# Six-layer local attention and MLP on one core: the third up-projection moved from slot 2 to slot 3, and the down-projection later in slot 3

## What is computed

```python
def local_attention(q, k, v):      # 16 heads of 64, windows of 32 tokens,
    ...                            # each window sees itself and the one before
def ffn_layer(x, g, bln, W1, b1, W2, b2):
    mu = x.mean(-1, keepdims=True)
    var = ((x - mu) ** 2).mean(-1, keepdims=True)
    xn = (x - mu) / jnp.sqrt(var + 1e-05) * g + bln
    hg = xn @ W1 + b1
    a, gate = jnp.split(hg, 2, -1)
    return a * jax.nn.gelu(gate, approximate=False) @ W2 + b2
for i in range(DEPTH):             # 6
    x = attn_layer(shift_tokens(x), Wqkv[i], ...) + x
    x = ffn_layer(shift_tokens(x), ln_g[i], ln_b[i], W1[i], b1[i], W2[i], b2[i]) + x
```

## Time and profile before

| | |
|---|---|
| median of 3 runs | 3688.08 us (3671.57 to 3697.3) |
| profiled execution, its own time | 3680.82 us |
| its span, first to last instruction | 3679.0 us |
| mean granted TensorE clock | 0.972 |
| TensorE matmuls busy | 93% of the span |
| TensorE weight loads busy | 67% |
| VectorE, ScalarE, GpSimd busy | 80%, 78%, 74% |

### The profile page before, as it was taken

How to read it: one execution, slowest core, us unless ns; L and a number is a source line. 1 busy time by engine, 2 the same in 40 slices (tenths; PEclk the granted TensorE clock), 3 DMA queues, 4 the chain that set the end, 5 groups by cost and what they waited for, 6 DMA issues and landing times. The chain is left out here.

```text
span 3679.0 us, 152268 instructions
## 1 busy us (share of the span) xinstructions
PE 3407.2 (93%) x62276; PEld 2469.7 (67%) x62276; DVE 2937.2 (80%) x4676; ACT 2873.9 (78%) x7344; POOL 2738.3 (74%) x3122
## 2 busy tenths in 40 slices
PE   8799999999999999998787799999999999999996
PEld 3477777777777777775232577777777777777774
DVE  7688888888888878884899688888788888888883
ACT  2488888888888888886665488888888888888884
POOL 3488888788888778873566588878788787888872
PEclk9899999999999999999899899999999999999998
DMA  1132333333332323322000132333333332333331
GB/s 41 50 79 74 83 78 77 78 83 74 84 80 73 84 72 78 82 72 69 1 0 1 42 74 74 81 80 75 75 81 75 82 81 68 88 76 76 81 74 37
DMA packets 182695, 251.35 MB, mean 68 GB/s; under 512 B 53364, under 2 KB 74360, under 8 KB 181880
## 3 DMA queue, kind: packets, MB, share of 16 engines
q1 hardware_dynamic: 182008, 241.65, 26.4%
HBM read 39.07 MB, written 1.05 MB: 11 GB/s over the span
## 5 line engine op out<-in xcount | busy, mean ns | idle before, releaser
L978 POOL TENSOR_TENSOR qk_rows<-rot_products 128x512 f32<-128x512 f32 x768 | 983.0, 1281 | 210.5 <-DVE rot_products L755 202.2
L755 DVE TENSOR_TENSOR rot_products<-psum,rot_scaled 128x1024 f32<-128x1024 f32 x768 | 937.2, 1220 | 158.0 <-ACT squares L538 131.4
L988 POOL TENSOR_TENSOR qk_rows<-qk_rows,rnorm 128x512 f32<-128x512 f32 x768 | 806.5, 1081 | 15.0
L272 PE MATMUL psum<-wqkv_hi,xs_hi 128*128 128x512 f32 x1152 | 561.6, 487 | 94.2 <-ACT gelu L622 41.7
L538 ACT ACTIVATE squares<-psum 128x512 f32<-128x512 f32 x768 | 505.8, 659 | 45.1 <-PE psum L274 39.7
L757 DVE TENSOR_REDUCE sumsq<-squares 128x8 f32<-128x512 f32 x768 | 518.7, 675 | 0.0
L546 ACT ACTIVATE v_rows<-psum 128x512 f32<-128x512 f32 x384 | 227.9, 595 | 324.6 <-DMA v_pairs<-v_rows 187.6
L346 PEld LDWEIGHTS psum<-probs_t,v_pairs 64*64 64x64 f32 x24576 | 395.4, 138 | 110.5 <-issue 110.1
L582 ACT ACTIVATE probs<-psum,minus_row_max 128x64 f32<-128x64 f32 x1536 | 457.2, 336 | 8.5 <-DVE minus_row_max L789 8.5
L274 PE MATMUL psum<-wqkv_hi,xs_lo 128*128 128x512 f32 x1152 | 461.9, 401 | 0.0
L273 PE MATMUL psum<-wqkv_lo,xs_hi 128*128 128x512 f32 x1152 | 461.5, 401 | 0.0
(11 more groups left out here) (189 smaller groups left out, 6167.9 us busy)
## 6 DMA issues: line engine op xcount, KB each, us to landing
v_pairs<-v_rows SPq DMA_DIRECT2D x3072, 64.0 KB, 2.0
wqkv_staged<-in_Wqkv SPq DMA_DIRECT2D x52, 384.0 KB, 3.9
wo<-in_Wo SPq DMA_DIRECT2D x12, 512.0 KB, 4.4
w<-in_W SPq DMA_DIRECT2D x12, 341.0 KB, 3.9
qk_scale<-in_qk_scale SPq DMA_DIRECT2D x12, 128.0 KB, 3.3
w<-in_W SPq DMA_DIRECT2D x12, 128.0 KB
mb_bc_pick<-in_mb_bc_pick SPq DMA_DIRECT2D x1, 1024.0 KB
out_x<-qk_rows SPq DMA_DIRECT2D x1, 1024.0 KB, 5.1
```

Of the source, the lines that this page charges most:

```text
L272: nc.tensor.matmul(proj_ps[c % 2], xh, wh, start=True, stop=False)
L755: V.tensor_tensor(m["mm"][:, c % 2, :, :].rearrange("p a (h e) -> p a h e", e=DH), ps, cos_sin, ALU.mult)\
L978: G.tensor_tensor(qk[:, c * CH:(c + 1) * CH].rearrange(half, a=2, e=DH // 2), cos, sin[:, :, ::-1, :], ALU.add)\
L988: G.tensor_tensor(part, part, m["rn"][:, u % 2, HC * c:HC * c + HC].unsqueeze(2) .to_broadcast([P, HC, DH]), ALU.mult).then_inc(S["rot_don ...
```

## The change

In the 45 iterations, up-projection 2 with its gelu and its multiplication goes from slot 2 to slot 3, to where the down-projection stood (behind chunk 3). The down-projection goes behind the second half of the scores, ahead of chunk 5. VectorE's two instructions after it go behind the softmax's two. The table is brought back in slot 3 too. `pe_pv_ready` of slot 2 now waits for hidden 1 in place of hidden 2; in slot 3 it waits for `stream` as before. `norm` is handed to it to keep the one odd iteration as it was.

```diff
@@ pe_pv_banks(e, u, norm)
+            elif u == 2 and norm:
+                nc.tensor.wait_ge(S["hidden_done"], e + 1)
             elif u == 2:
-                nc.tensor.wait_ge(S["hidden_done"], e + 1)
+                nc.tensor.wait_ge(S["h_done"], 2 * e + 2)
             else:
                 nc.tensor.wait_ge(S["stream"], B + e + 1)
@@ pe_up
-            if j < 2:
-                nc.tensor.wait_ge(S["d1_ev"], added_)
+            nc.tensor.wait_ge(S["d1_ev"], added_)
@@ pe_body
-                if mlp and u in (1, 2):
+                if mlp and (u in (1, 2) or u == 3 and not norm):
                     pe_up(it - 1, u - 1, added_)
-                if mlp and u == 3 and not norm:
-                    pe_down(it - 1, added_)
                 pe_probs_t(it, u, nxt)
@@
-                if mlp and u == 2:
+                if norm and u == 2:
                     pe_up(it - 1, 2, added_)
                 if nxt:
                     pe_scores(it, u + 1, 1)
+                if mlp and u == 3 and not norm:
+                    pe_down(it - 1, added_)
@@ act_body
-                if mlp and u in (1, 2):
+                if mlp and (u in (1, 2) or u == 3 and not norm):
                     act_gelu(it - 1, u - 1)
@@
-                if mlp and u == 2:
+                if norm and u == 2:
                     act_gelu(it - 1, 2)
-                if mlp and u in (1, 2):
+                if mlp and u in (1, 2, 3) and not (norm and u == 3):
                     nc.scalar.preload_act_table_set("natural_log_exp_and_others")
@@ dve_body
                 if mlp and u == 3 and not norm:
-                    dve_down(it - 1)
+                    dve_hidden(it - 1, 2)
                 if proj:
                     dve_rnorm(it, u + 2)
-                if mlp and u == 2:
+                if norm and u == 2:
                     dve_hidden(it - 1, 2)
                 if nxt:
                     dve_softmax_in(it, u + 1)
+                if mlp and u == 3 and not norm:
+                    dve_down(it - 1)
```

More of the change, by code:

```diff
@@ L352, in pe_pv, with pe_pv_ready @@
                                 last.then_inc(S["o_mm"], 1)
-        def pe_pv_ready(it, u, mlp, alone):
+        def pe_pv_ready(it, u, mlp, alone, norm):
             nc.tensor.wait_ge(vp_sem[u % TILES], it * PAIRS + PAIRS * (u // TILES + 1))
@@ L361, in pe_pv_ready, with pe_pv_banks @@
             if mlp:
-                pe_pv_banks(it - 1, u)
-        def pe_pv_banks(e, u):
+                pe_pv_banks(it - 1, u, norm)
+        def pe_pv_banks(e, u, norm):
             if u == 0:
@@ L498, in pe_body @@
                     pe_proj(it, u + 2, 5, two)
-                pe_pv_ready(it, u, mlp, norm and u == 3)
+                pe_pv_ready(it, u, mlp, norm and u == 3, norm)
                 if ahead or u + 3 < TILES:
```

## The result

The changed kernel takes **3714.75 us** (median of 4 runs, 3710.67 to 3731.59) against 3684.51 us for the kernel before (4 runs, 3671.57 to 3697.3). The ratio is 1.0091, with a 95% interval of 1.0063 to 1.0119, which does not hold 1. The change costs about 0.9%: 30 us between the medians, 34 us by the ratio. The forecast was 3682 us, no change that can be measured.

The account below looks back on a forecast made before the run. TensorE's own queue was taken as the bound. Slots 3, 2 and 0 gave +2.98 - 1.65 - 1.5 = -0.17 us an iteration, -6.5 us in all with the last iteration; forecast 3682 us, range 3652 to 3724.

Parts of the forecast that it names:

- a stall behind `stream` in slot 3: Slot 3: with the down-projection late, TensorE's chunk 0 waits for VectorE's additions, a new 1.26 us in each iteration.
- slot 0's gain: Slot 0: SP starts its 16 DMAs 1.26 us earlier, so v0 is less late; gain 1.5 us, at most 1.75.
- 14.8 + 0.45 = 15.3: Slot 0: 14.8 us plus 1.0 us per us of v0's lateness, with 0.45 us of lateness left, gives 15.3 us.
- slot 3's: Slot 3: 15.77 plus the up-projection's 1.72 and the stall's 1.26 us gives 18.75, a loss of 2.98 us.
- chunk 0 starts at T + 4.64: Slot 3, T the down-projection's start: VectorE starts 2.81 after T, needs 1.51, and chunk 0 follows 0.32 us later.
- the four long slots 0: Slot 0 before: four slots with mean 19.4 us where the line gives 17.3, put down to the granted clock falling.
- rival 2: Slower: slot 0 gains nothing, the DMAs being late otherwise or short slot 2 passing lateness on; 3748 us, chance 0.08.
- Slot 2 (15.53 for 15.5): Slot 2: loses up-projection 2 and the wait for hidden 2, falling from 17.13 to 15.5 us, a gain of 1.65.
- three signs of being wrong: Stall under 0.8 or over 1.7 us; slot 0's v0 over 1 us late; a 0.5 clock in windows after the stall.
- No price for the tables: Slot 3, ScalarE: two more table loads cost nothing, since 1.28 us of load fits in ScalarE's idle time.
- Rival 1: Slower: TensorE's clock falls behind slot 3's new stall, 2.1 us each fall; 3774 us with all 44, chance 0.10.
- a sum of three terms: Per iteration: slot 3 +2.98, slot 2 -1.65, slot 0 -1.5, together -0.17 us, by 44 iterations -7.5 us.

Follow-up runs that it names:

- the three reorderings: Logarithm ahead of v0, TensorE's bank wait behind chunk 0, slot 1's table back ahead of v0: kernel before 3626.68 us, changed kernel 3668.31 us.
- experiment 3: The changed kernel with the third gelu as Identity and so no table loads in slot 3: 3711.41 us, ratio 1.0109.

## Why the prediction was wrong, and where it was right

The mechanism was right: a stall behind `stream` in slot 3, and a slot 0 that gets back what slot 3 loses. What failed is the size of terms in the sum that was to come out near nothing (-0.17 us an iteration forecast, +0.63 measured). The largest is slot 0's gain, put at 1.5 and measured at 1.17: its step "14.8 + 0.45 = 15.3" left out the wait that ends last once the DMAs are in time. Next come slot 3's, 2.98 for 3.25, which had the stall nearly right and no term for TensorE's stops, and slot 1's, which was put at nothing and measured +0.15. The terms nearly cancel, and each of four errors went the same way: 0.27 in slot 3, 0.05 in slot 2, 0.33 in slot 0 and 0.15 in slot 1, together 0.80 us an iteration. By 44 that is 35 of the 41.6 us between the forecast of the span (-6.5) and what came (+35.1).

**Slot 3, the stall: 1.34 us, not 1.26.** The step "chunk 0 starts at T + 4.64" was three durations laid end to end, and over the 42 iterations two of them hold: the handover to chunk 0 has a median of 0.32 (0.31 to 0.51), as forecast, and the additions take 1.52 for 1.51. VectorE starts 2.88 behind T, not 2.81. That is all of the 0.08. The iteration of the rows above, with a handover of 0.41, is one of the longer ones.

**Slot 3, the tail.** Its median over the 42 is 18.81, and 15.69 + 1.72 + 1.34 = 18.75: the two terms explain it but for 0.06. Its mean is 19.01, 0.2 above. In 8 of the 42 slots 3 the stretch from chunk 0 to chunk 1 takes 3.8 to 4.4 us, where the median is 2.86; before, the longest four were 3.35 to 3.80. The row of one of them:

```profile
1077.33 1.71 PE L346 MATMUL psum<-probs_t,v_pairs 64*64 64x32 f32 x102
1079.84 0.65 PE L346 MATMUL psum<-probs_t,v_pairs 64*64 64x32 f32 x26 [0.80 <-issue]
```

TensorE stops within its run of 128 small matmuls, and no semaphore accounts for it. The trace's record of transfers says more. The page of the profile has a DMA queue for instructions, with 497 transfers of 16 KB in either kernel (queue, transfers, MB, share):

```profile
q8 instruction: 497, 8.14, 1.0%
```

In the 13 kept traces there are 576 such stops of over 0.25 us in this run of matmuls. Every one of them ends 1.16 to 1.66 us after the end of a transfer of that queue; of all the matmuls of these runs 10% start within such a stretch. The likeliest reading is that TensorE waits there for its own instructions. It rests on the times alone; no run moved these transfers.

The waits of the program put the stops of this line at 33.1 us in 47 times before, 41.2 in 58 after. With 12 DMAs it is 19.9 and 28.5, with the three reorderings 30.0 and 40.1. Part of that is only moved from other lines: over all of TensorE's lines the waits called "issue" are 41.9 and 45.6, 32.3 and 38.7, 32.8 and 46.5. They were more in the changed kernel of all three pairs, by 4 to 14 us. Why they are more with this order stays open: no run tried it.

**Slot 0: 15.63, not 15.3.** The lateness fell to 0.31, further than the 0.45 of the forecast, so the mechanism did its part in full. What failed is "14.8 + 0.45 = 15.3". The line was drawn through slots that were nearly all late (the shortest lateness was 0.35) and was used at its end. Another wait stands there. TensorE's chunk 2 writes a bank that VectorE's rotation of chunk 0 (line 756) must have read, and VectorE, which has the norm's work in this slot, is late with it:

```profile
569.53 0.47 PE L272 MATMUL psum<-wqkv_hi,xs_hi 128*128 128x512 f32 x1 [0.68 <-DVE rot_products L756]
```

That is 0.49 us a slot 0 over the 42 (22 waits), where it was 0.19 before (10 waits); the stops described above are 0.18. The shortest slot 0 is 14.98, and 14.98 + 0.49 + 0.18 = 15.65, for 15.62 measured. The kernel before with 12 DMAs gives the slot with no lateness, 15.43 in the mean, with 0.31 of the same wait in it. So against the 16.93 before (16.80 in the 20 iterations), the gain was bounded at about 1.4 to 1.5, whatever the stall did.

The forecast also misread one of its rows here. Of the four long slots 0 that it put down to the clock, three show a lower granted clock (0.82 to 0.83 over the slot). The fourth, 18.30 us long, has 1.00, and in it TensorE waited 1.70 us for this same rotation. And a part of slot 0's gain is the clock after all: over the 42, seven slots 0 of the kernel before show a fall, and none in the changed kernel. The seven are 19.33 us long in the mean and the other 35 are 16.45, which is 0.48 us an iteration, the longer waits ahead of the falls included.

**Slot 1: +0.15, not 0.** The prediction took it as unchanged. Slot 1's lateness went from 0.29 to 0.40 and slot 3's from 0.05 to 0.71. With 12 DMAs, where nothing is late, slot 1 has +0.06. Its v0 hangs on the DMAs of slot 0's v1, and a shorter slot 0 leaves SP's 11 us of issuing less time; that this is the cause of the rest is argued from the order, not tried. Slot 3's lateness costs nothing that the traces show: with 12 DMAs and none of it the slot has the same median, 18.81. If so, lateness was passed on by the very slot that got rid of it, which is what rival 2 said of slot 2.

**Right.** Slot 2 (15.53 for 15.5), with some luck: over the 42 it is 15.57, and that holds two slots of 19.93 in the mean in which the granted clock fell, for which the forecast had no term; the others have 15.35. The stall's row in each of the 42, 50.2 us together for "45 to 55", though under another name than line 839. The wait for the logarithm (1.4 us for "under 15"). None of the three signs of being wrong came: the stall is between 0.8 and 1.7, v0 of slot 0 is 0.31 late, and no clock fell behind the stall. No price for the tables: 45 more loads on each line and 2.5 and 2.4 us of idle time ahead. The Trainium skill ("ScalarE: Activation LUTs", What ACT_TABLE_LOAD costs) counts a drain of about 1.38 us with each. This case does not show it: 1283 ns and then the gelu 0.01 us later (803.32, 804.61), and experiment 3. Rival 1, the clock, did not come: all 42 slots 3 and the slots 0 that follow have a mean granted clock of 0.99 or more, that is the full 2.4 GHz. Two windows just behind the stall, one of them in the slot of 1077.33:

```profile
812.22:819.22 7.00, 6.93 (x158) 5.83 (x159) 3.82 (x5) 6.04 (x25) 3.25 (x4) 1.00 0.36 88
1076.47:1083.47 7.00, 6.20 (x152) 5.33 (x152) 3.81 (x5) 6.03 (x25) 3.14 (x4) 1.00 0.33 80
```

**The sum.** The time is within the range (3652 to 3724), but the chance of 0.70 for "no change" was for a sum of three terms, each with its own error of 0.1 to 0.3 us, multiplied by 44. An error of 0.5 us is 22 us. That the time still fell within it is no merit of the sum, whose sign was wrong. The errors may have had a common sign for a reason: where a gain has a floor (slot 0 can't be shorter than its work and its other waits) and a loss has none (a tail), the likeliest value of the sum lies above that of its parts. That is argued; this case is one instance.

## What to carry to other kernels

When two terms nearly cancel, bound each by its floor before adding them: don't extend a line beyond its data, and ask which wait ends last once the one you remove is gone (here VectorE's rotation, 31.9 us already before). An operation moved closer to its consumer costs its whole answer (matmuls, two handovers, VectorE's additions), and cover is what TensorE does between: here 0.8 us of cover in place of 2.6 was a stall of 1.34 us in each iteration. If a stall seems to pay for itself by relieving another wait, look at what stands in the queue behind that wait: moving the logarithm ahead of v0 gave 0.67 us in slot 0 for nothing, where the change paid 1.34 us for 1.17. And take such durations over all iterations: one iteration said 1.43.

## What the runs showed of the hardware

- The name that the profile gives to a wait's end can be the wrong one of two that come close. It said ScalarE's v1, which ended 0.24 us before VectorE's addition; with that addition shorter, chunk 0 started in the middle of v1.
- The handover from VectorE's end to TensorE's start, for one pair of lines, had a median of 0.32 us over 42 instances, and a range of 0.31 to 0.51.
- An idle time of 1.16 to 1.38 us in TensorE, in each of 42 iterations, left its granted clock alone there (0.99 or more in the slots 3 and the slots 0 behind them; 0.974 for the whole kernel, 0.972 before). Behind waits of 1.64, 1.70 and 2.06 us in slots 0 of the kernel before it fell.
- A queue's issuing is a resource. SP takes 11.31 us for 16 DMAs (median 11.11), of the 15 to 17 us of a slot. Four fewer in a tile took 8.39 and made the kernel before 2.4% faster, though the DMA share was only 0.24 to 0.39 and the last landing came no sooner after its issue (1.44 and 1.40 us).
- TensorE can stop for some tenths of a us, up to 2.3, within a run of small matmuls with no semaphore to wait for. All 576 such stops of over 0.25 us in the 13 traces end 1.16 to 1.66 us behind the end of a 16 KB transfer of the instruction queue. How often it happens changed with the order of the program.
